# Softmax row sums of layer 0 taken over pairwise added exponentials, on one Trainium2 core

## What is computed

```python
Q = _split_heads(x, H)
K = _split_heads(x @ Wk + bk, H)
V = _split_heads(x @ Wv + bv, H)
causal = jnp.tril(jnp.ones((S, S), dtype=bool))
mask = jnp.where(causal, 0.0, -jnp.inf).astype(x.dtype)
scores = jnp.einsum('bhqd,bhkd->bhqk', Q, K) + mask
attn = jax.nn.softmax(scores, axis=-1)
o = jnp.einsum('bhqk,bhkd->bhqd', attn, V)
o = o.transpose(0, 2, 1, 3).reshape(B, S, -1)
return x + jax.nn.gelu(o, approximate=False) @ Wf + bf
```

## Time and profile before

| | us |
|---|---|
| median of 3 runs | 2564.33 |
| the three runs | 2559.43, 2564.33, 3105.05 |
| profiled execution, its own time | 2583.99 |
| its span from first to last instruction | 2582.2 |

### The profile page before, as it was taken

One profiled execution on the slowest core, in us unless ns is written; L12 is line 12 of the kernel. 1 busy time (PEld: TensorE's weight loads), 2 busy tenths in 40 slices (PEclk: granted clock), 3 DMA queues, 4 the chain that ended last, 5 costly groups with the idle time before them and its releaser, 6 DMA issues. The chain is left out here.

```text
span 2582.2 us, 30828 instructions
## 1 busy us (share of the span) xinstructions
PE 2217.8 (86%) x11109; PEld 873.0 (34%) x11109; DVE 1486.7 (58%) x3043; ACT 1343.8 (52%) x1923; POOL 833.9 (32%) x909
## 2 busy tenths in 40 slices
PE   6799976779999998778999999777899999877789
PEld 2233432234433342223443344222343334322243
DVE  6562556856556266675656445677565635577552
ACT  2345447962244635795225553688423454378922
POOL 1112125533411313562331221365142122146534
PEclk7899977879999986588999998767899999766889
DMA  5200231004310023100520022110051002401013
GB/s 145 67 15 18 67 99 36 1 1 119 101 28 2 21 78 83 36 1 13 143 72 20 2 66 80 36 36 1 23 156 42 20 2 83 98 9 27 1 53 88
DMA packets 67850, 128.38 MB, mean 50 GB/s; under 512 B 11397, under 2 KB 24837, under 8 KB 63077
## 3 DMA queue, kind: packets, MB, share of 16 engines
q1 hardware_dynamic: 67696, 126.40, 17.9%
HBM read 109.99 MB, written 15.20 MB: 48 GB/s over the span
## 5 line engine op out<-in xcount | busy, mean ns | idle before, releaser
L1281 DVE TENSOR_REDUCE mx<-ps 128x1 f32<-128x512 f32 (+3 forms) x992 | 612.5, 655 | 373.8 <-PE ps L620 241.3
L1029 ACT ACTIVATE pr<-ps 128x1024 f32<-128x1024 f32 (+3 forms) x672 | 515.0, 804 | 404.3 <-PE ps L690 403.7
L690 PE MATMUL ps<-qop,kop 75*128 75x512 bf16 (+7 forms) x1344 | 407.6, 367 | 123.1 <-DVE wb L1343 41.5
L617 PE MATMUL ps<-kop,qop 72*128 72x512 bf16 (+6 forms) x1248 | 425.4, 374 | 92.1 <-DVE mx L1281 69.7
L1572 POOL TENSOR_SCALAR_AFFINE_SELECT pr<-pr 128x512 f32<-128x512 f32 x224 | 145.5, 649 | 730.9 <-ACT pr L1029 730.1
L736 PE MATMUL ps<-pr,vt 128*32 128x512 f32 (+3 forms) x2688 | 340.4, 584 | 8.2 <-POOL pr L1572 7.6
L1090 ACT ACTIVATE pr<-ps 128x512 f32<-128x512 f32 x224 | 133.8, 597 | 337.6 <-PE ps L846 273.7
L617 PEld LDWEIGHTS ps<-kop,qop 72*128 72x128 bf16 (+1 forms) x1248 | 128.1, 105 | 424.9 <-DVE mx L1281 256.1
L690 PEld LDWEIGHTS ps<-qop,kop 75*128 75x128 bf16 (+1 forms) x1344 | 121.6, 104 | 361.7 <-ACT pr L1029 117.9
L856 PE MATMUL ps<-pr,w_down 128*128 128x512 f32 x384 | 196.7, 599 | 4.1 <-POOL pr L1563 4.1
L843 PE MATMUL ps<-hT,w_gate 128*128 128x512 f32 x384 | 196.2, 592 | 0.2 <-DVE on L1508 0.2
(11 more groups left out here) (316 smaller groups left out, 3153.0 us busy)
## 6 DMA issues: line engine op xcount, KB each, us to landing
wb<-gates_scratch SPq DMA_DIRECT2D x192, 256.0 KB, 3.4
kop<-kparts_scratch SPq DMA_DIRECT2D x32, 576.0 KB
qop<-qparts_scratch SPq DMA_DIRECT2D x96, 192.0 KB
on<-hmax_scratch SPq DMA_DIRECT2D x8, 1024.0 KB, 5.7
kparts_scratch<-on SPq DMA_DIRECT2D x12, 256.0 KB, 2.9
qparts_scratch<-on SPq DMA_DIRECT2D x12, 256.0 KB, 4.9
qparts_scratch<-wb SPq DMA_DIRECT2D x12, 192.0 KB
kparts_scratch<-wb SPq DMA_DIRECT2D x12, 192.0 KB
```

What stands on the lines that cost most here:

```text
L617: mm = pe.matmul(o, qop[0:k, slot(l, u), j, qb * P:(qb + 1) * P], kop[0:k, slot(l, u), j, k0:k0 + wd], start=True, stop=not diag)
L690: mm = pe.matmul(o, kop[0:k, slot(l, u), 2 * pair + j, kb * P:(kb + 1) * P], qop[0:k, slot(l, u), 2 * pair + j, q0:q0 + wd], start=True, s ...
L1029: nc.scalar.activation(pr[:, g % 3, 2 * pair:2 * pair + 2, o0:o0 + wd], ps[:, bank:bank + 2, o0:o0 + wd], ACT.Exp).then_inc(a.exps, 1)
L1281: ins_ = nc.vector.tensor_reduce(mx[:, nth(l, u) % 2, j0:j0 + heads, qb, col % 2], ps[:, bank, 0:heads * wd].rearrange("p (j n) -> p j n", ...
```

## The change

Two neighbouring steps 2k and 2k+1 have the same chunk and therefore add into the same row sums. Instead of eight matmuls with ones over the two, the exponentials of step 2k+1 are added onto those of step 2k (on the columns that step 2k+1 has), and four matmuls with ones run over the sum (`sums(k)` on PE). A unit has six pairs. The pairs (0,1), (2,3), (8,9) and (10,11) are masked, and DVE adds them in one instruction over four heads, of 4x384 or 4x128 elements a partition; the pairs (4,5) and (6,7) are full, and POOL adds them in two instructions of 2x512 elements. The add overwrites the buffer of step 2k, so it waits for the values matmuls of that step (`pv`), and for the cut of step 2k+1 or its exponentials.

The ring of buffers grows from three to five: the three of `pr` and the two halves of `wb` (`probs`). `sums(k)` stands at position 2k + 4, at the head of the position. The exponential of step g waits for the sums that free its buffer. `sums_out` and `scale_out` move from positions 4 and 0 of a unit to positions 7 and 3. Five semaphores of the prologue are shared with other uses; the instructions there are as before.

The core of the diff:

```diff
+        def probs(l, g):
+            if l:
+                return pr[:, g % 3]
+            return (pr[:, 0], pr[:, 1], pr[:, 2], wb[:, 0], wb[:, 1])[g % RING0]
...
                     for j in range(4):
                         h = 4 * u + j
                         mm = pe.matmul(ps[32 * j:32 * j + 32, 4, o0:o0 + wd], vt[:, kb, 32 * h:32 * h + 32],
-                                       pr[:, g % 3, j, o0:o0 + wd], start=kb == 0, stop=last,
+                                       probs(l, g)[:, j, o0:o0 + wd], start=kb == 0, stop=last,
                                        tile_position=(0, 32 * j))
-                    if l == 0:
-                        for j in range(4):
-                            mm = pe.matmul(ps[32 * j:32 * j + 32, 5, o0:o0 + wd], ones32[:],
-                                           pr[:, g % 3, j, o0:o0 + wd], start=kb == 0, stop=last,
-                                           tile_position=(0, 32 * j))
-                        mm.then_inc(a.pv, 1)
+                    mm.then_inc(a.pv, 1)
+
+                def sums(k):
+                    u, s = divmod(2 * k, NS)
+                    c, kb, q0, wd, _ = STEPS[s]
+                    o0 = q0 - c * CH
+                    if masked_pair(k):
+                        pe.wait_ge(a.added[0], pairs_until(k, True))
+                    else:
+                        pe.wait_ge(a.added[1], 2 * pairs_until(k, False))
+                    if kb == 0 and k:
+                        pe.wait_ge(a.s_out, NC * u + c)
+                    for j in range(4):
+                        mm = pe.matmul(ps[32 * j:32 * j + 32, 5, o0:o0 + wd], ones32[:],
+                                       probs(0, 2 * k)[:, j, o0:o0 + wd], start=kb == 0, stop=kb == 4 * c + 2,
+                                       tile_position=(0, 32 * j))
+                    mm.then_inc(a.sums, 1)
...
+                    if l == 0 and p % 2 == 0 and 4 <= p:
+                        sums(p // 2 - 2)
                     if p + 1 < steps:
                         scores(p + 1, extra)
...
+                    sums(NS * UNITS // 2 - 1)
                     pe.wait_ge(a.exps, 2 * NS * UNITS)
                     idle(2, 13)
...
+                        if l == 0 and g >= RING0:
+                            act.wait_ge(a.sums, (g - RING0) // 2 + 1)
+                        elif l and g >= 3:
                             act.wait_ge(a.pv, g - 2)
...
-                        if s == 4:
+                        if s == 7:
                             sums_out(u, 0)
-                        if s == 0 and u:
+                        if s == 3 and u:
                             sums_out(u - 1, 1)
...
+                def add_pair(k):
+                    even, odd = pair_halves(k, slice(0, 4))
+                    dve.wait_ge(a.cut, diagonals(2 * k + 2))
+                    dve.wait_ge(a.pv, 2 * k + 1)
+                    nc.vector.tensor_tensor(even, even, odd, ALU.add).then_inc(a.added[0], 1)
...
+                    adding = l == 0 and p and p % 2 == 0 and masked_pair(p // 2 - 1)
+                    first = len(SIDE[l, more][p]) // 2 if shift != NOBODY or adding else 99
                     for x in SIDE[l, more][p][:first]:
                         side_job(*x)
...
+                    if adding:
+                        add_pair(p // 2 - 1)
                     for x in SIDE[l, more][p][first:]:
                         side_job(*x)
...
+            def add_pair(k):
+                pool.wait_ge(at[0].exps, 2 * (2 * k + 2))
+                pool.wait_ge(at[0].pv, 2 * k + 1)
+                for heads in (slice(0, 2), slice(2, 4)):
+                    even, odd = pair_halves(k, heads)
+                    nc.gpsimd.tensor_tensor(even, even, odd, ALU.add).then_inc(at[0].added[1], 1)
...
                 cut(0, g)
-                if g % NS == 4:
+                if g % 2 and not masked_pair(g // 2):
+                    add_pair(g // 2)
+                if g % NS == 7:
                     scale_out(g // NS, 0)
-                if g % NS == 0 and g:
+                if g % NS == 3 and g >= NS:
                     scale_out(g // NS - 1, 1)
```

More of the change, by code:

```diff
@@ L16 @@
 HYP_RING = 5
+RING0 = 5
 PAIRS = 3 * HD * 3
@@ L395, in hyp_z, with masked_pair, pairs_until, pair_halves @@
             return z[:, :, q0 - c * CH:q0 - c * CH + wd]
+        def probs(l, g):
+            if l:
+                return pr[:, g % 3]
+            return (pr[:, 0], pr[:, 1], pr[:, 2], wb[:, 0], wb[:, 1])[g % RING0]
+        def masked_pair(k):
+            return STEPS[(2 * k + 1) % NS][4]
+        def pairs_until(k, masked):
+            return sum(masked_pair(i) == masked for i in range(k + 1))
+        def pair_halves(k, heads):
+            _, _, q0, wd, _ = STEPS[(2 * k + 1) % NS]
+            o0 = q0 % CH
+            return [probs(0, 2 * k + i)[:, heads, o0:o0 + wd] for i in range(2)]
         fa, fh = pr[:, 1, 0:3], pr[:, 2, 0:3]
@@ L452, in __init__ @@
                 self.pv = sem(n + "pv")
+                if l == 0:
+                    self.added = [sem(n + "added_dve"), sem(n + "added_pool")]
+                    self.sums = sem(n + "sums")
                 self.o_out = sem(n + "o_out")
@@ L731, in values @@
                             pe.wait_ge(a.o_out, out_before(u, c))
-                            if l == 0:
-                                pe.wait_ge(a.s_out, NC * u + c)
                     for j in range(4):
@@ L972, in sums_out @@
                     i = NC * u + c
-                    act.wait_ge(a.pv, NS * u + 4 + 8 * c)
+                    act.wait_ge(a.sums, (NS * u + 4 + 8 * c) // 2)
                     if i >= 2:
@@ L1026, in std_exp @@
                         act.wait_ge(a.scores, 2 * g + pair + 1)
-                        if g >= 3:
+                        if l == 0 and g >= RING0:
+                            act.wait_ge(a.sums, (g - RING0) // 2 + 1)
+                        elif l and g >= 3:
                             act.wait_ge(a.pv, g - 2)
-                        nc.scalar.activation(pr[:, g % 3, 2 * pair:2 * pair + 2, o0:o0 + wd],
+                        nc.scalar.activation(probs(l, g)[:, 2 * pair:2 * pair + 2, o0:o0 + wd],
                                              ps[:, bank:bank + 2, o0:o0 + wd], ACT.Exp).then_inc(a.exps, 1)
@@ L1376, in attention @@
                         hyp_arg(hyp_at(p - 1))
-                    first = len(SIDE[l, more][p]) // 2 if shift != NOBODY else 99
+                    adding = l == 0 and p and p % 2 == 0 and masked_pair(p // 2 - 1)
+                    first = len(SIDE[l, more][p]) // 2 if shift != NOBODY or adding else 99
                     for x in SIDE[l, more][p][:first]:
@@ L1569, in cut @@
                 if diag:
-                    past = pr[:, g % 3, :, q0 - c * CH:q0 - c * CH + P]
+                    past = probs(l, g)[:, :, q0 - c * CH:q0 - c * CH + P]
                     pool.wait_ge(at[l].exps, 2 * (g + 1))
@@ L1835, in next_batch @@
             nc.all_engine_barrier(sems_to_clear=range(first_sem, last_sem + 1))
-        s_mod = ctx.enter_context(nc.semaphore("s_mod"))
-        s_silu = ctx.enter_context(nc.semaphore("s_silu"))
-        s_mm = ctx.enter_context(nc.semaphore("s_mm"))
+        s_mod = tables
+        s_silu = sq_ready
+        s_mm = ss_ready
         s_ready = ctx.enter_context(nc.semaphore("s_ready"))
-        s_consts = ctx.enter_context(nc.semaphore("s_consts"))
+        s_consts = t_col
         with nc.Block() as block:
```

3 lines of the change are left out of this document (removed).

## The result

The changed kernel takes 2555.28 us (median of 20 runs), the kernel before 2567.38 us beside it, a ratio of 0.9963 with a 95% interval of 0.9946 to 0.9981: 9.5 us faster, 5 to 14. The ratio leaves out three much longer executions (3105 us before; 3845 and 10324 us after), while the two medians, which are 12.1 us apart, include them. The forecast was 7.6 us faster.

The account below looks back on a forecast made before the run. PE's own instructions were taken to set the pace. A batch element saves 5.8 us, less 3.9 us for clock falls: 1.9 us, 7.6 us in all, from 2564.3 to 2556 us, with a range of 2518 to 2594.

Parts of the forecast that it names:

- PE's relief: Row sums on PE, all 16 units: 3.54 us less a unit, 56.6 us in all, not all on the path.
- Positions 0 to 7: Unit with pieces, from its scores to step 7's values: 1.9 us saved, bounds -0.7 and 2.4.
- The border: Between two units, from the end of step 7's values to the next unit's scores: 0.84 us saved.
- The first unit: First unit of a batch element, without sums of a unit before it: 1.1 us more saved than the others' 2.7.
- Unit 3, B: From the end of step 6's values to step 8's values, behind POOL's queue: 4.55 us becomes 7.8, 3.2 lost.
- Unit 3, A: From unit 3's first scores to the end of step 6's values: 1.54 us less sums, 1.0 counted as saved.
- Unit 3, C: From step 8's values to the last Ln: 6.27 us becomes 7.4, 1.2 lost.
- Unit 3 as a whole: Unit 3 from first scores to last Ln: 3.4 us longer, before any fall of the clock.
- The clock: TensorE's clock: 1.5 falls of 2.57 us, 3.9 us a batch element; one in unit 3, half for three borders.
- The rule of the Trainium skill: Clock falls at each of three borders and in unit 3, four falls; as first rival 26 us slower, chance 0.2.
- The DVE adds: Positions 0 to 7: adds of 1.76 and 0.69 us; DVE load 15.9 us against PE's 16.10, 0.5 us seen.
- rival 2: DVE becomes the bound in units with pieces, all 3.14 us of adds seen: 18 us slower, 2582 us; chance 0.12.

Follow-up runs that it names:

- no_adds: Changed kernel without any adds on DVE or POOL; row sums run over the even steps' exponentials only: ratio 0.9815, 2518.26 us.
- fill: Changed kernel with 12 idle matmuls of zeros on PE ahead of the wait for step 8's cut in unit 3: ratio 0.9928, 2545.98 us.
- all_dve: Changed kernel with every pair in all units added by DVE and the last add ahead of the last copy: ratio 1.0178, 2614.08 us.
- pool_only: Changed kernel without adds on DVE; masked pairs' sums run over both steps, POOL's adds of full pairs stay: ratio 1.0017.
- best: Changed kernel with unit 3's full pairs added by DVE, last add before the last copy, and `scale_out` one step later: ratio 0.9902, 2537.09 us; repeated, 0.9858.
- unit3_dve: Changed kernel with unit 3's full pairs added by DVE instead of POOL, other units unaltered: ratio 0.9864, 2533.87 us.
- again: The changed kernel unaltered, timed and profiled a second time: ratio 0.9956 to the kernel before, 2552.64 us.

## Why the prediction was right

The sign and the size hold, the size in part by luck: wrong terms offset each other, as the end of this section says. Step by step, per batch element:

- **PE's relief.** Half the row sum matmuls, as said: 768 of 1536 records. That not all 56.6 us are on the path holds too: no_adds, which pays for nothing, gains 1.85% (47 us; 45 by the medians).
- **Positions 0 to 7** saved 1.8 us in units 1 and 2 (29.4 us from scores to the end of step 7's values, about 31.2 before), forecast 1.9.
- **The border** saved 0.3 us, forecast 0.84. From L648 to the scores it is 3.74 us (157.66 to 161.40), before 3.71; the saving lies ahead of L648, 6.35 us (from 151.31) against 6.68, and these two are the same at all twelve borders of each profile. So the leftover pieces gained less from their earlier start than they could. Why is left open. Units 1 and 2 so give 2.1 us each in the best case and 1.8 on average, not 2.7.
- **The first unit** gave 4.4 us, forecast 3.8. A part of it is the clock: before, all four first units ran at 0.91 to 0.93; after, two of them kept 1.00 (40.2 and 41.0 us). At 0.93 before and 0.92 after it is 46.1 and 42.3 us, a saving of 3.8.
- **Unit 3, B**: 7.4 us from the end of step 6's values (839.16) to step 8's (846.55); forecast 7.8. POOL's add takes 2358 ns, forecast 2365. Right in mechanism and size.
- **Unit 3, A**: 822.68 to 839.16 is 16.5 us, 2.0 saved where 1.0 was forecast: the allowance for ACT was too large. The 0.67 us that PE waits at 829.95 were not in the term.
- **Unit 3, C**: 846.55 to 855.52 is 8.97 us, forecast 7.4. In the kernel with PE's wait filled it is 7.46 us, so the term itself was right, and the difference is the clock. The tail's order (copy, add, sums) costs 0.76 us, shown by moving it.
- **Unit 3 as a whole** loses 2.0 us at a clock of 1.00 (31.34 in fill against 29.33), forecast 3.4; the difference is A's, and 0.4 of B.
- **The clock** was the most mis-sized term: I counted 3.9 us. B's wait brought a fall in all four batch elements, as forecast, at 2.0 us on average and not 2.57 (1.5 to 2.7, by the table under fill). The borders were given half a fall; of the eight units 1 and 2 one fell (41.76 us at 0.96, against 39.5), and no unit 3 fell before B's wait. And the kernel before had a fall of its own in one unit 3 of four, 0.6 us a batch element, which I left out of the comparison. So unit 3 lost 3.4 us against before with its falls included (33.4 against 30.0), forecast 3.4 + 2.6. The rule of the Trainium skill ("TensorE: Matmul & The Clock Gate", What's actually happening) that I set against the change, four falls by it, held at one place of four, B's, where PE had 3.13 us to wait; all_dve, with 3 us of waiting at each border, ran at 0.83 to 0.87 in eleven of twelve units.
- **The DVE adds** take 1.75 and 0.68 us (forecast 1.76 and 0.69), and the load does fit by a hair: rival 2's mechanism is real, and begins as soon as 4.58 us more are put on DVE. Its chance of 0.12 was for the change as made, and there it stayed away.

Two slips of arithmetic in the prediction change nothing: rival 2's terms add to -4.5 us and not -4.6, and B's wait of 3.2 us is 3.4 times 0.95 us and not four times.

Without the clock the measured terms are 2 x 2.1 + 3.8 - 2.0 = 6.0 us, forecast 5.8: the saving at a border was forecast 0.5 us too high, three times, and the loss in unit 3 1.4 us too high, and the two offset each other. That is luck. With the clock the two profiles give a saving of 4.4 + 2 x 1.8 - 3.4 = 4.6 us, 18.6 us in all, where 7.6 was forecast and the times say 9.5 us. So the forecast of the time is nearer than its terms are. The 9 us between profiles and times are left open: the profiled execution of before had a lower granted clock than its others, and in the twelve profiled runs other than before, median less loops gives anything from 1926 to 1939 us, where it should be one number, so one profile doesn't tell a sum over 16 units closer than that.

## What to carry over

Before work is moved to an idle engine, look at what stands behind it in that engine's own queue: in unit 3 POOL was busy 8.6 of 32 us, and still adds of 4.7 us a pair ahead of a cut of 0.64 us made the unit 33.4 us long, where it is 28.8 with the same adds on DVE. Choose the engine for each stage, by what is free there (DVE in unit 3, POOL elsewhere), and not once for the whole loop. And a busy share of 74% on DVE already set the end where bursts of reductions had to be done before PE might go on; what PE then waited came back a second time through its clock. Filling such a wait with idle matmuls (fill) gave the clock's part back, 2.0 us a batch element, but not the wait.

## What the hardware showed that I had not expected

**POOL all but stops while DVE adds two tensors of SBUF.** The cuts of the kernel after, against the earlier trace rows, and those of the kernel without adds on DVE (pool_only):

```profile
L1617 POOL TENSOR_SCALAR_AFFINE_SELECT pr<-pr 128x512 f32<-128x512 f32 x176 | 131.6, 748 | 427.7 <-ACT pr L1064 427.4
L1626 POOL TENSOR_TENSOR pr<-pr 128x1024 f32<-128x1024 f32 x32 | 74.8, 2358 | 52.8 <-PE ps L756 41.1 <-ACT pr L1064 11.7
L1617 POOL TENSOR_SCALAR_AFFINE_SELECT wb<-wb 128x512 f32<-128x512 f32 x48 | 40.3, 839 | 66.3 <-ACT wb L1064 66.2
```

```profile
L1615 POOL TENSOR_SCALAR_AFFINE_SELECT pr<-pr 128x512 f32<-128x512 f32 x176 | 116.0, 659 | 441.9 <-ACT pr L1064 441.5
L1615 POOL TENSOR_SCALAR_AFFINE_SELECT wb<-wb 128x512 f32<-128x512 f32 x48 | 30.5, 636 | 73.5 <-ACT wb L1064 73.5
```

The mean hides that only some cuts are slow: in the four loops 36 of 128 take over 0.70 us in the kernel after, and none in pool_only and in no_adds, which have no add on DVE. (The few slow ones left in pool_only's mean lie outside these loops.) Four slow instructions of POOL can be laid beside the DVE add in the timelines above (a cut alone is 0.64, a scaling 1.28 us):

```
                         together   POOL longer by
after, cut at 159.19       0.68 us      0.55 us
after, cuts at 828.60      0.81         0.68
best, cut at 842.46        1.00         0.85
unit3_dve, scaling 838.41  1.08         0.93
```

In the time that both run, POOL gets on by about a sixth; in the slowest cuts of the kernel after, 2.01 us long with 1.52 us beside the add, by a tenth. DVE isn't slowed (1.74 to 1.76 us each time). POOL's adds beside DVE's reductions, which read PSUM, keep their 2.35 us. The Trainium skill ("GPSIMD Engine Reference", 1. Specifications) says that POOL shares its SBUF interfaces with VectorE and contends with its instructions that have two SBUF inputs; the trace agrees, and adds the size. Here it costs what hangs on a cut: 0.24 us at 160.42 and 0.67 us at 829.95.

**The same wait cost TensorE's clock two different amounts.** B's wait is 3.13 us each time, and behind it the clock of unit 3 is 0.95 in five batch elements of the two profiles (after, again), at a cost of 1.5 to 1.6 us, and 0.90 in three, at 2.4 to 2.9 us. The fall of the earlier trace rows fits the second group, 0.89 and 2.57 us, though it came behind a wait of 0.95 us. So in these units a fall costs by how long TensorE is left at 1.2 GHz, which the granted clock of the unit tells: 0.95 is a tenth of it, 0.90 a fifth. The length of the wait doesn't tell it; what decides between the two is left open.
